# Moving the first-layer attention's score units, keep-warm matmuls, weighting steps and one small transfer in a two-layer kernel on one core

## The reference

```python
qkv = x @ w_qkv + b_qkv                       # 16 heads, Dh = 8, T = 512
att = einsum('bhqd,bhkd->bhqk', q, k) / sqrt(Dh)
att = softmax(where(causal, att, -inf), axis=-1)
y = einsum('bhqk,bhkd->bhqd', att, v)
x = x + ga * (y.reshape(b, t, c) @ w_proj + b_proj)
```

## Time and profile before

| | |
|---|---|
| median of 3 runs | 2838.94 us |
| lowest and highest | 2838.05 and 2848.37 us |
| time of the profiled execution | 2848.37 us |
| its span, from first to last instruction | 2846.6 us |
| mean granted TensorE clock | 0.971 of full speed |
| TensorE busy | 2462.7 us, 87% |
| VectorE busy | 1851.1 us, 65% |
| ScalarE busy | 1532.9 us, 54% |
| GpSimd busy | 863.1 us, 30% |

### The profile page before, as it was taken

One profiled execution on the slowest core, in us unless ns is written; L12 is line 12 of the kernel. 1 busy time (PEld: TensorE's weight loads), 2 busy tenths in 40 slices (PEclk: granted clock), 3 DMA queues, 4 the chain that ended last, 5 costly groups with the idle time before them and its releaser, 6 DMA issues.

```text
span 2846.6 us, 66899 instructions
## 1 busy us (share of the span) xinstructions
PE 2462.7 (87%) x24434; PEld 1709.5 (60%) x24659; DVE 1851.1 (65%) x4760; ACT 1532.9 (54%) x3241; POOL 863.1 (30%) x609
## 2 busy tenths in 40 slices
PE   3888988889898998979989898898988889888898
PEld 2546755467553775548755477555774567654676
DVE  3467763777637776477665776557865678646776
ACT  0476444755348554485444755447544674446653
POOL 2045210452105521064201552025420353204521
PEclk8999999999999999999999999999999999999999
DMA  7101131011310103001140012200131011310112
GB/s 230 62 4 19 16 102 57 4 19 16 102 57 7 20 11 122 38 11 17 23 142 5 12 17 54 110 4 13 19 99 66 1 18 17 95 66 2 18 17 98
DMA packets 233090, 128.77 MB, mean 45 GB/s; under 512 B 177999, under 2 KB 220375, under 8 KB 225783
## 3 DMA queue, kind: packets, MB, share of 16 engines
q1 hardware_dynamic: 227910, 118.16, 15.0%
q10 hardware_dynamic: 4836, 6.03, 0.6%
HBM read 86.98 MB, written 37.13 MB: 44 GB/s over the span
## 4 chain that ended last, share of the span: by engine, by line
PE 48%; DVE 18%; ACT 12%; issue 10%; DMA 5%; POOL 4%; SPq 3%; DVEq 0%; POOLq 0%; ACTq 0%
PE bank L880 6%; PE bank L675 4%; PE bank L666 3%; ACT arena L1599 3%; DVE small L1332 3%; PE bank L598 3%; PE bank L979 3%; PE bank L485 2%; PE bank L523 2%; PE bank L956 2%; ACT vq L1607 2%; DVE mx L1136 2%; PE bank L918 2%; DVE blk_t L1334 2%; PE bank L909 2%
## 5 line engine op out<-in xcount | busy, mean ns | idle before, releaser
L485 PE MATMUL bank<-mask_k,ident_bf 128*128 128x512 bf16 x1248 | 315.5, 384 | 23.7 <-issue 15.2
L1280 DVE SCALAR_TENSOR_TENSOR arena<-bank,conv,arena 128x510 f32<-128x510 f32 (+1 forms) x384 | 284.3, 747 | 56.8 <-ACT arena L1600 33.1
L1848 POOL TENSOR_TENSOR arena<-arena 128x511 f32<-128x511 f32 x192 | 243.6, 1272 | 182.0 <-DVE arena L1280 181.1
L1856 POOL TENSOR_TENSOR arena<-upto,gk 128x1536 f32<-128x1536 f32 x32 | 88.2, 2755 | 674.4 <-DVE beta L1273 674.4
L741 PE MATMUL bank<-h_t,arena 128*128 128x512 f32 x384 | 207.6, 633 | 64.9 <-DVE arena L1280 64.9
L1136 DVE TENSOR_REDUCE mx<-bank 128x2 f32<-128x768 f32 (+3 forms) x187 | 202.0, 1124 | 57.3 <-PE bank L524 55.7
L485 PEld LDWEIGHTS bank<-mask_k,ident_bf 128*128 128x128 bf16 x1400 | 128.9, 99 | 150.4 <-issue 21.8
L1563 ACT ACTIVATE arena<-bank 128x384 f32<-128x384 f32 (+1 forms) x384 | 168.2, 545 | 45.9 <-PE bank L583 45.9
L523 PE MATMUL bank<-vq 128*128 128x128 bf16 (+3 forms) x528 | 123.0, 318 | 54.4 <-issue 34.2
L1332 DVE TENSOR_TENSOR small<-blk_t,blk 96x1 f32<-96x1 f32 (+14 forms) x480 | 149.4, 311 | 16.5
L741 PEld LDWEIGHTS bank<-h_t,arena 128*128 128x128 f32 x384 | 60.6, 191 | 152.3 <-DVE arena L1280 139.1
(11 more groups left out here) (294 smaller groups left out, 5906.4 us busy)
## 6 DMA issues: line engine op xcount, KB each, us to landing
vq<-q_rows SPq DMA_DIRECT2D x18, 1024.0 KB, 9.2
vq<-k_rows SPq DMA_DIRECT2D x18, 1024.0 KB, 11.6
arena<-w_bounce SPq DMA_DIRECT2D x16, 1024.0 KB, 6.3
q_rows<-qkp SPq DMA_DIRECT2D x81, 128.0 KB, 2.4
k_rows<-qkp SPq DMA_DIRECT2D x81, 128.0 KB, 2.4
arena<-in_L_attn_Wv_dram SPq DMA_DIRECT2D x8, 768.0 KB, 10.3
t<-t_bounce SPq DMA_DIRECT2D x256, 12.0 KB, 1.8
x<-t_bounce SPq DMA_DIRECT2D x256, 12.0 KB, 1.8
```

Of the source, the lines that this page charges most:

```text
L485: mm(PS[bank][:, :], ident_bf[:, :], mask_k[:, :, :].rearrange("p h w -> p (h w)"), start=True, stop=True)
L1280: ins = V.scalar_tensor_tensor(a[:, k:T], ps[:, 0:T - k], conv[:, n, 3 - k:4 - k], a[:, k:T], ALU.mult, ALU.add)
L1848: G.tensor_tensor(acc[:, n % 4, 1:T], acc[:, n % 4, 1:T], acc2[:, n % 3, 0:T - 1], ALU.add).then_inc(taps_added, 1)
```

## The change

It has five parts.

1. The twelve keep-warm matmuls around `move_maxima(b, 1, 0)` at the loop's end go; the four after unit NU + 1 at its beginning become ten.
2. Units NU + 2 to NU + 5 are issued ahead of head 0, and the rest is interleaved anew. `move_maxima(b, 0, 1)` directly follows `weigh(0)`, ahead of head 5.
3. `weigh(1)` follows head 8 (was: head 10) and `weigh(2)` head 12 (was: head 13); `turn(0)` follows head 9 and `turn(1)` follows `weigh(2)`. ScalarE's copies follow heads 4, 8 and 12.
4. `weigh(g)` waits once for all twelve exponentials of its four heads. In before it waits for the first lot of its last head, and for the other two lots as it comes to them.
5. SyncE issues the five weight loads ahead of `maxima(b, 0, 1)` and no longer after it.

```diff
@@ weigh(g), TensorE
+                    pe.wait_ge(p_ready, at(b, p_ready, 12 * g + 12))
                     c0 = 0
                     for j in range(NT):
-                        if j < 3:
-                            pe.wait_ge(p_ready, at(b, p_ready, 12 * g + 10 + j))
@@ the order of the attention, TensorE
                 scores(b, 0, NU)
                 scores(b, 0, NU + 1)
-                keep_warm(1, 4)
-                for h in range(5):
-                    scores_t(h)
-                    scores(b, 0, NU + 2 + 2 * h)
-                    if h < 4:
-                        scores(b, 0, NU + 3 + 2 * h)
+                keep_warm(1, 10)
+                for u in range(NU + 2, NU + 6):
+                    scores(b, 0, u)
+                scores_t(0)
+                scores(b, 0, NU + 6)
+                scores_t(1)
+                scores(b, 0, NU + 7)
+                scores_t(2)
+                scores(b, 0, NU + 8)
+                scores(b, 0, NU + 9)
+                scores_t(3)
+                scores(b, 0, NU + 10)
+                scores_t(4)
                 weigh(0)
-                scores_t(5)
                 move_maxima(b, 0, 1)
-                scores_t(6)
-                scores_t(7)
-                for h in range(8, 11):
+                for h in range(5, 9):
                     scores_t(h)
                 weigh(1)
+                scores_t(9)
                 turn(0)
-                for h in range(11, 14):
+                for h in range(10, 13):
                     scores_t(h)
                 weigh(2)
                 turn(1)
-                for h in range(14, HA):
+                for h in range(13, HA):
                     scores_t(h)
                 turn(2)
                 weigh(3)
@@ the loop's end, TensorE
                     scores(b, 1, 3 + FT + t)
-                keep_warm(7, 8)
                 move_maxima(b, 1, 0)
-                keep_warm(7, 4)
@@ after the exponentials of head h, ScalarE
-                    if h in (4, 10, 13):
-                        copy_y((4, 10, 13).index(h))
+                    if h in (4, 8, 12):
+                        copy_y(h // 4 - 1)
@@ SyncE, after the gates
-                maxima(b, 0, 1)
                 sp.wait_ge(weights_out, 32)
                 sp.dma_start(w1t.rearrange("p n m -> p (n m)"), w1_bounce).then_inc(w_in, 16)
                 sp.dma_start(w2t.rearrange("p n m -> p (n m)"), w2_bounce).then_inc(w_in, 16)
...
                 sp.dma_start(wconv[:, 2 * nq:2 * nq + nv], L1_attn_Wv).then_inc(wc_in, 16)
+                maxima(b, 0, 1)
                 tokens(b, 1)
```

## The result

| | before | after |
|---|---|---|
| median, same chip | 2838.49 us (4 runs) | 2875.74 us (4 runs) |
| lowest and highest | 2835.4 and 2848.37 us | 2865.3 and 2879.0 us |
| ratio, 95% interval | | 1.0118 [1.0084, 1.0154] |
| the profiled execution's span | 2846.6 us | 2858.8 us |
| mean granted clock in it | 0.971 | 0.972 |

The change costs 1.2%, some 33 us (24 to 44 by the interval; the two medians alone lie 37 us apart). The prediction was 24 us and 2863 us. The two profiled executions are only 12 us apart, since that of before is the slowest of its four and that of after is, at 2860.56 us, shorter than all four timed ones, at a higher clock than theirs (0.972 against 0.966 to 0.969). What differs between the two is found outside the attention: there the execution of before is 15 us longer over the seven stretches between one attention and the next.

The account below looks back on a forecast made before the run. No engine bounds the kernel everywhere; TensorE, 48% of the chain, is full from T8 to `weigh(3)`. Per sample 0.5 + 0.35 + 2.25 = 3.1 us, times 8 is 24.8, less 1: +24, 2863 us; range 2832 to 2881.

Parts of the forecast that it names:

- its own forecast: Whole kernel: the predicted slowdown's own range, 2855 to 2872 us, given a chance of 0.5.
- three signs of being wrong: Gap at copy_y(1) hidden; R earlier than S + 5.8; or the clock elsewhere changing by more than this stage.
- R: VectorE's restart at its third unit after the loop's edge; claimed S + 6.8, coming 0.5 us later per sample.
- S: TensorE's start of the next sample's scores at the loop's edge; claimed 0.5 us sooner.
- The weightings: Parts 3 and 4, T8 to weigh(3): claimed 14.5 us against 12.25, +2.25 us per sample.
- the walk: Step-by-step count through the engines' queues from R, then T8; claimed T8 = R + 16.45 and weigh(3) at 14.5.
- T8: Start of head 8's first exponential on ScalarE; claimed at R + 16.45.
- `weigh(2)`'s new place: After head 12, between T8 and weigh(3): claimed to cost 0.7 to 0.8 us of the 2.25.
- half clock at every start: At all edges TensorE starts S at clock 0.50; claimed to last 4 to 6 us, taken as 5.
- R to T8: Part 2, from VectorE's restart to head 8's exponentials: claimed 16.45 us, +0.35; bounds 0 and +1.0.
- The loads: Part 5, SyncE's earlier weight loads: claimed 0 us.
- The 1 us that the sum took off for the read-back: The maxima's read-back, alone in the queues after part 5: claimed gain of 1 to 2 us in all.

Follow-up runs that it names:

- early_half: The changed kernel with parts 3 and 4 undone; ratio to before 1.0063 [1.0043, 1.0082].
- late_only: The kernel before with part 3 alone, staged waits kept; ratio to before 1.0010 [0.9991, 1.0029].
- wait_only: The kernel before with part 4 alone, one wait per weighting; ratio to before 1.0024 [1.0003, 1.0046].
- staged_back: The changed kernel with part 4 alone undone, waits staged again; ratio to before 1.0077 [1.0054, 1.0099].
- warm4: The changed kernel with four keep-warm matmuls at the beginning in place of ten; ratio to before 1.0085 [1.0062, 1.0108].
- edge_back: The changed kernel with the twelve keep-warm matmuls at the loop's end put back; ratio to before 1.0098 [1.0076, 1.0120].
- edge_only: The kernel before without the twelve keep-warm matmuls at the loop's end; ratio to before 1.0044 [1.0020, 1.0069].
- loads_only: The kernel before with part 5 alone, the early weight loads; ratio to before 1.0010 [0.9988, 1.0033].
- unit_first: The kernel before with unit NU + 2 in place of the four keep-warm matmuls after NU + 1; ratio to before 0.9958 [0.9942, 0.9975].
- unit_turn: unit_first plus the early weight loads and the turn directly after weigh(0); ratio to before 0.9961 [0.9940, 0.9982].

## Why the prediction was right, and where it was off

The direction, the path and the largest term were right; the size was short, 24 us for 33, and the time of 2876 us lies within the full range of 2832 to 2881, but just above the 2855 to 2872 that it gave to its own forecast. None of its three signs of being wrong came: the gap at `copy_y(1)` is open, R is never sooner than S + 5.9, and the stretches outside the attention differ by 15 us between the two traces where the attention differs by 32.

**The weightings (parts 3 and 4).** +2.25 us foretold, 2.17 measured, with each stall where the walk put it: 1.45 ahead of the copy of group 1, 1.22 (1.1 foretold) ahead of that of group 2, and `weigh(3)` 14.4 us after T8. Shown by early_half, late_only, wait_only and staged_back. The split was off: I gave 0.7 to 0.8 to `weigh(2)`'s new place, but that is the single wait's second payment. The argument that a full TensorE can only get gaps from a new order held: 14.65 us of work and 14.69 now.

**The restart R (part 1).** +1.0 for the step foretold, +0.83 measured; half clock at every start foretold and seen. Shown by warm4: the ten matmuls are what the maxima wait for. By the runs, the six more of them cost 1.29 us (warm4), the twelve that went 0.41 (edge_back), and the rest of the change, with head 0 no longer ahead of R, gives back some 0.9.

**The start S, the step that failed.** The prediction had "I take -0.5 us for S" and the first score came no sooner (0.12 us later in the mean, within the spread of kernels that are the same there). The time from the turn to the first score is 3.7 to 4.4 us whether four matmuls stand in it or none. I had read the 3.08 us behind the last weight load as what follows the dispatch of the last matmul. The runs fit a jump that begins once the turn is issued, with the matmuls running beside it; edge_only, where nothing else was changed, has 4.06 us from the turn to the first score. The traces say more. At each of the 98 edges (seven in each of fourteen kernels) one transfer of 16 KB starts on instruction queue 8 between the turn and the first score. It starts 1.0 to 1.8 us after the turn, 1.14 in the median both with the four matmuls and without them, and the first score follows its landing by 1.6 to 1.9 us everywhere. So what the first score follows is this transfer, and the four matmuls do not delay its start. No run changed the transfer itself. The prediction also weighed, and did not follow, what the Trainium skill states, that TensorE's queue is 64 deep ("TensorE: Matmul & The Clock Gate", section "Architectural detail"). What it drew from that, that the removed four are worth nearly nothing, agrees with this trace, which shows 3.79 us with the four and 3.73 without in sample 2; how deep the queue is no run shows. That failed 0.5, with the 0.12, is 5 us of the 33.

**R to T8 (part 2).** +0.35 foretold and +0.89 measured (1.1 without the long read-back in before's mean), a term of the right sign and too small. The walk had `weigh(0)` start at R + 9.1; it starts at R + 9.62 in every sample. By the start times of sample 1, TensorE loses some 0.15 us within head 1 behind ScalarE, 0.2 ahead of NU + 9 behind VectorE, and 0.2 from head 4 to `weigh(0)`, of which half is put down to ScalarE; I had none of them in full. From `weigh(0)` on the walk holds: 7.35 us foretold to T8, 7.38 measured. This is 4 us of the 33. No run has part 2 alone: that the step belongs to it follows from the others, since R to T8 stays at 17.0 us with part 1 taken back (warm4, edge_back), with parts 3 and 4 taken back (early_half), and is 16.0 with part 5 alone.

**The loads (part 5).** 0 foretold, none seen (loads_only). The 1 us that the sum took off for the read-back rests on the one sample of the earlier trace rows, and no run bears it out.

The sum of the four terms was 3.1 us per sample, and 4.0 were measured; two misses of 0.6 and 0.5, less 0.2 for R and 0.1 for the weightings. The two executions' spans differ by only 12 us, which would have hidden two thirds of the effect from a reader of spans alone.

## What to carry to other kernels

Where an engine's stretch is full, as TensorE's here with 14.65 us of work in 15.10, a new order of the same work can only lose; look for the stretch in which the leading engine is idle behind something, and put the next real work there, as unit_first did with a unit in place of keep-warm matmuls. An engine that waits once for all its inputs, where it could start on the first, costs nothing where the inputs are long there, and costs at each place where it stands right behind its producer (0.77 us here at one such place, 1.53 at two), so such a wait and such a move must be priced together. When two executions of one program differ by more than the effect sought, compare the same stage, sample by sample: here the step from T8 to `weigh(3)` was steady to 0.02 us while the whole varied by 20.

## What the runs showed of the hardware

**Keep-warm matmuls at a loop's end did not lengthen it.** The jump back holds TensorE idle for 2.6 to 3.2 us behind four matmuls and for 3.5 to 4.1 behind none, and the first score comes equally late. In all fourteen traces it comes 1.6 to 1.9 us after a 16 KB transfer of the instruction queue has landed, which itself starts 1.0 to 1.8 us after the last instruction that waits for a semaphore, the turn.

**The clock falls within the edge in every sample once nothing runs in it.** In after it is at full speed at 771, at 0.50 at 773 and back in the window at 779. Before, with the twelve matmuls, it was at half for the first score in some samples and at full speed in others, and in sample 6 it never fell at the edge. Taking twice the shortfall of the mean granted clock as the time at 1.2 GHz, the attention of samples 1 to 7 holds 48 us of it in each of the five kernels without the twelve, and 20 to 41 in the nine that have them (27 in before, 24 in edge_back).

**The whole kernel's clock goes with the twelve too.** The mean granted clock over a kernel's timed runs is 0.967 to 0.969 in each of the five without them, and 0.971 to 0.976 in each of those that have them, before included. On the chip of edge_only it is 0.968 over ten runs against 0.976 over the 31 of before, some 42 us more at half speed, of which the attention holds about 20. The other 22 could cost at most half of that, 11 us. That edge_only's 12 us come from there is argued from this, not shown.

**Half-speed stretches elsewhere go with the spread of single executions.** The seven stretches outside the attention (from `weigh(3)` of samples 0 to 6 to the next edge) hold 68 to 99 us at half clock, and are 2135 to 2161 us long. The code in them is the same in all fourteen kernels, but for the eight keep-warm matmuls at their end. Before has 99 us and 2161, after 79 us and 2146, loads_only 68 and 2138, wait_only 72 and 2136. The relation is loose (unit_turn has 96 us and 2148), as it would be if half clock cost nothing where TensorE isn't the bound; no run tests it.
